# Full attention in reversed row order, with GpSimd marking zeros and the value sums made beforehand; router pieces moved in the windowed stage

## The chip, the cores and the metric

The kernel runs on one core of one Trainium2 chip. A core has five engines with instruction streams of their own: TensorE (PE in the profile; PEld is its weight load), VectorE (DVE), ScalarE (ACT), GpSimd (POOL) and SyncE (SP), and DMA queues. Each engine works through its stream in order and waits on semaphores. The metric is the device time of one execution in microseconds (us), as a median of several.

## The reference

A hidden state x of 2 x 2048 tokens by 128 features passes through four blocks in float32: windowed attention with 16 heads, a mixture of experts, full attention, and the same mixture of experts again. Each block adds to x what it makes of the normalised x. The change touches the routing of both mixtures and the full attention:

```python
# routing, before each mixture of 8 experts
logits = xf @ w_router
probs = jax.nn.softmax(logits, axis=-1)
topk_w, topk_idx = jax.lax.top_k(probs, 2)

# full attention: one head of width 128, 2 sequences of 2048
scores = jnp.einsum('bqd,bkd->bqk', q, k) / jnp.sqrt(jnp.float32(d_k))
scores = jnp.triu(scores, k=0)                       # a query sees itself and LATER keys
scores = jnp.where(scores == 0, -9000000000000000.0, scores)
attn = jax.nn.softmax(scores, axis=-1)
out = jnp.einsum('bqk,bkd->bqd', attn, v)
```

A zero score counts as masked, with a large finite value, so the masked keys ahead of a query still enter the sum with the weight that the softmax gives them.

## The kernel before, in words

Tokens lie in 32 tiles of 128 rows, in 8 groups of 4 tiles (512 tokens). The stages run one after the other; each is a block in which every engine has its own loop, written out by hand, and no scheduler moves anything.

**Windowed attention** (`window_stage`). `turn(sb, routed)` handles group sb: for each of 8 pairs of heads (c) it goes through 4 blocks (b), 32 steps (c, b) in all. Its first turn carries no routing, and the other seven route the group before (sb - 1) beside the attention. In a step PE makes scores (L627), transposes of probabilities (L637), one projection and the product with V (L650). DVE adds the mask and takes the extremum for the score tile made three steps ahead (L812, `maxima`), ACT exponentiates it (L734) and copies the transposes (L742). PE writes the next score tile only when `maxima` has emptied the bank, so a late DVE stops PE. In b = 1 and 2 DVE also swaps halves and multiplies by the cosine (L821, L825) for the rotary embedding, and POOL multiplies by the sine and adds (L962, L969), copies (L977, L984, L987), and every pair's last POOL work runs into the next pair's b = 0.

**The router** (`Router`) is a chain of small steps over one group of four tiles: `statistics` and `normalise` on DVE with a square root on ACT between them (`root`, L322, which needs another function table than the exponential), `turn` and `logits` on PE, `shift` on DVE, `exponentials` on ACT, `order`, `choose` and `accumulate` on DVE, `count` on PE, `assign` and `slots` on DVE, then on POOL `second` (L433, a copy) and `scatter` (L441, 8 indirect DMAs, two for each tile). Most DVE steps are links: an operation, then a wait for its own semaphore. In the windowed stage the step at which each piece runs is a pair (c, b) compared by hand: ROOT (2, 2), `normalise` (3, 0), TURN (3, 2), LOGITS (4, 0), EXPS (4, 1), `order` (4, 3), `choose` (5, 0), `accumulate` (5, 3), COUNT with `assign` and `slots` (6, 1), and the scatters in c = 6 and 7, four DMAs each. At LOGITS and COUNT PE waits for both halves of the latest score tile, since the small products share its bank.

**Full attention** (`full_stage`). For each of two batches: 12 projections (L1325, L1329), then 16 rows i of query tiles. Row i has the key tiles i to 15, cut into chunks of up to four tiles: 40 chunks in a batch, 136 tiles of scores. The rows go from i = 0 (four chunks) to i = 15 (one tile). The loop over chunks g is a pipeline:

- PE: `turn(g)` transposes the probabilities (L1347), `scores(g + 7)` (L1338), `values(g - 1)` multiplies by V (L1356). With the first chunk of each row it sums the value tile that has just become masked, by a product with ones (L1376).
- ACT: `copy(g + 6)` (L1415) takes the scores out of PSUM into U, `exponentials(g + 1)` (L1422, L1425), `read(g)` (L1432) copies the transposes.
- DVE: `take(g + 6)`: for a row's first chunk the triangle (L1492), then over the whole chunk u = (u == 0) - u (L1493) and a minimum over it (L1495); on the row's last chunk the bias for the exponential (L1498, L1499). `finish` of a row that is done (L1507 to L1523): add the new value sum to `pre`, add its masked share to the product, divide, add to x.
- POOL: the routing's copy and scatters only.

The bias of a row needs all chunks of it, and `values` of a row's first chunk waits until the row before the last has been finished.

The routing of the second mixture is spread over this loop: `ROUTE_AT[j]` is the chunk (of 80 over both batches) at which group j of finished rows begins, and STATS to SLOTS are steps 0 to 6 after it. Before the change the groups begin at 17, 29, 37, 45, 57, 69, 77 and 82; what is at 80 or later runs after the last chunk. PE's `routed` waits for a step's reader before the bank `pt` is written again. After the last scatter has landed the second expert stage starts.

## Time and profile before

| What | us |
|---|---|
| median of 3 runs (1600.51 to 1601.87) | 1601.13 |
| the profiled execution | 1602.77 |
| its span, from first to last instruction | 1601.0 |
| PE busy in the span | 1288.1 (80%) |
| DVE busy | 1065.4 (67%) |
| ACT busy | 912.0 (57%) |
| POOL busy | 787.3 (49%) |
| mean granted TensorE clock | 0.914 |

The shares are averages over stages with different limits. By the line numbers in the trace the windowed attention runs from about 57 to 843 us, the first expert stage from 875, the full attention from 1098 to 1398 and the second expert stage after it. A wait in the profile is idle time of one engine, with the engine whose signal ended it. "DVEq" is DVE's sequencer, which signals without an operation. The granted clock is a share of TensorE's 2.4 GHz.

### The profile page before, as it was taken

The numbers are of one execution on the slowest core, as the hardware profiler recorded it, in microseconds if no ns is written. First come the engines' busy times: TensorE is split into PE (matmuls) and PEld (weight loads), VectorE is DVE, ScalarE is ACT, GpSimd is POOL, SyncE is SP. The second block draws the span as 40 slices with busy tenths as digits, with TensorE's granted clock in tenths as the row PEclk, the third lists the DMA queues.
The fourth block names the chain that finished last, engine by engine and source line by source line (L and its number), as shares of the span: only waits on it lengthen the run. The fifth ranks groups of instructions, "written<-read, shape, count | busy, mean of one in ns | idle before, by whom it ended". The sixth has DMA issues, their size and how long they took to land. (4 is left out here: it accounts for less than half of the span.)

```text
span 1601.0 us, 34670 instructions
## 1 busy us (share of the span) xinstructions
PE 1288.1 (80%) x9684; PEld 1012.3 (63%) x9684; DVE 1065.4 (67%) x3751; ACT 912.0 (57%) x2312; POOL 787.3 (49%) x814
## 2 busy tenths in 40 slices
PE   0599999999999999999981888916978887188891
PEld 0477766766667676676751788913765666188891
DVE  5666777777767678776774455656886878445563
ACT  1377776768678686776852544513764666044450
POOL 4356667666676756757662344510022223434451
PEclk9899999999999999999995989967999899598896
DMA  5699994000000000000003112130000000121215
GB/s 191 120 210 205 202 207 90 1 9 6 1 15 0 15 1 7 8 1 15 1 12 135 58 54 59 56 106 0 1 14 14 14 16 25 34 64 55 59 57 158
DMA packets 129390, 91.84 MB, mean 57 GB/s; under 512 B 9115, under 2 KB 122030, under 8 KB 128992
## 3 DMA queue, kind: packets, MB, share of 16 engines
q1 hardware_dynamic: 118848, 71.32, 20.8%
q0 software_dynamic: 9248, 16.94, 3.2%
q10 hardware_dynamic: 1152, 2.13, 0.4%
q14 instruction: 106, 0.87, 0.2%
q8 instruction: 36, 0.59, 0.2%
HBM read 30.86 MB, written 61.64 MB: 58 GB/s over the span
## 5 line engine op out<-in xcount | busy, mean ns | idle before, releaser
L812 DVE CUSTOM_DVE_ANT_0 sc<-ps,mask 128x256 f32<-128x256 f32 x518 | 198.2, 420 | 155.8 <-PE ps L627 135.0
L734 ACT ACTIVATE sc<-sc,mx 128x256 f32<-128x256 f32 x516 | 257.6, 503 | 45.9 <-DVE mx L812 45.3
L962 POOL TENSOR_TENSOR rot<-rot,sin 128x512 f32<-128x512 f32 x132 | 180.3, 1366 | 202.0 <-DVE rot L821 202.0
L1107 POOL DMA_INDIRECT yt<-yo,xt x160 | 160.5, 1003 | 196.7 <-DVE yo L1207 168.1
L441 POOL DMA_INDIRECT xg<-r_xw,r_slot x128 | 127.5, 996 | 161.7 <-DVE r_slot L418 127.5
L627 PE MATMUL ps<-K,Q 64*128 64x256 f32 x1036 | 192.0, 433 | 15.7 <-DVE mx L812 15.7
L742 ACT COPY pT<-pt 128x512 f32<-128x512 f32 x257 | 150.3, 585 | 95.1 <-PE pt L637 86.5
L1167 ACT ACTIVATE hT<-ph,b 128x256 f32<-128x256 f32 x320 | 125.7, 477 | 86.6 <-PE ph L1130 86.6
L637 PE MATMUL pt<-ident,sc 128*128 128x128 f32 x1028 | 171.3, 290 | 1.6 <-ACT sc L734 1.3
L650 PE MATMUL po<-pT,V 128*64 128x128 f32 x2048 | 168.3, 285 | 0.0
L637 PEld LDWEIGHTS pt<-ident,sc 128*128 128x128 f32 x1028 | 109.9, 143 | 85.7 <-issue 52.0
L1148 PE MATMUL py<-w2s,hT 128*128 128x128 f32 x1280 | 161.6, 281 | 1.9 <-ACT hT L1167 1.8
L1148 PEld LDWEIGHTS py<-w2s,hT 128*128 128x128 f32 x1280 | 155.8, 198 | 2.7 <-ACT hT L1167 2.7
L650 PEld LDWEIGHTS po<-pT,V 128*64 128x64 f32 x2048 | 106.5, 136 | 65.9 <-issue 35.9
L1130 PE MATMUL ph<-xh,w1s 128*128 128x256 f32 x640 | 143.6, 307 | 0.0
L627 PEld LDWEIGHTS ps<-K,Q 64*128 64x128 f32 x1036 | 85.8, 186 | 61.1 <-issue 37.4
L1130 PEld LDWEIGHTS ph<-xh,w1s 128*128 128x128 f32 x640 | 112.5, 204 | 0.0
L825 DVE TENSOR_TENSOR lin<-lin,cos 128x512 f32<-128x512 f32 x132 | 108.0, 818 | 0.0
L734 ACT ACTIVATION_READ_ACCUMULATOR sc<-sc,mx 128x1 f32 x516 | 99.0, 192 | 0.0
L1162 ACT CAST xh<-px 128x256 fp32r<-128x256 f32 x80 | 29.9, 374 | 120.1 <-PE px L1121 78.3
L821 DVE STREAM_SHUFFLE rot<-lin 128x512 f32<-128x512 f32 x132 | 96.9, 734 | 0.2
L1189 DVE CAST w1s<-w1h 128x512 fp32r x80 | 34.0, 424 | 91.1 <-issue 90.1
(236 smaller groups left out, 2826.3 us busy)
## 6 DMA issues: line engine op xcount, KB each, us to landing
xg<-zeros SPq DMA_DIRECT2D x76, 520.0 KB, 10.1
xt<-xg SPq DMA_DIRECT2D x80, 130.0 KB, 2.1
got<-yt SPq DMA_DIRECT2D x32, 256.0 KB, 4.5
yt<-yo,xt POOLq DMA_INDIRECT x160, 2.3
x<-in_hidden SPq DMA_DIRECT2D x8, 256.0 KB, 8.2
xg<-r_xw,r_slot POOLq DMA_INDIRECT x128, 2.3
w<-in_w SPq DMA_DIRECT2D x1, 2048.0 KB, 8.7
out_x<-x SPq DMA_DIRECT2D x8, 256.0 KB, 3.9
```

The lines of the kernel that those rows point to most:

```text
L441: self.nc.gpsimd.indirect_dma_start(out=rows, out_offset=bass.IndirectOffsetOnAxis(ap=self.slot[:, self.buf(g), r, t:t + 1], axis=0), in_= ...
L627: ins = nc.tensor.matmul(ps[:, h, 0:2 * P], Q[r, c % QBUF, b * P:(b + 1) * P], K[r, c, b * P:(b + 2) * P], start=True, stop=True)
L637: ins = nc.tensor.transpose(pt[:, b % 2, h, kb, :], sc[:, b, h, kb * P:(kb + 1) * P], s.ident[:, :])
L650: ins = nc.tensor.matmul(po[h * HD:(h + 1) * HD, c % 2, b * P:(b + 1) * P], V[:, c, b + kb, h, :], pT[:, b % 2, h, kb, :], start=(kb == 0) ...
L734: nc.scalar.activation(sc[:, b, h, :], sc[:, b, h, :], ACT.Exp, scale=-1.0, bias=mx[:, b, h:h + 1], accum_out=ls[:, c % 2, b, h:h + 1]).th ...
L742: nc.scalar.copy(pT[:, b % 2, :, :, :], pt[:, b % 2, :, :, :]).then_inc(S["pt"], 1)
L812: nc.vector.tensor_tensor_reduce(sc[:, b, h, :], ps[:, h, 0:2 * P], (mask0 if b == 0 else mask)[:, :], -float(HD) ** -0.5, 3e38, ALU.add, ...
L962: nc.gpsimd.tensor_tensor(rot[:, which, :], rot[:, which, :], s.sin[:, pos(sb)], ALU.mult).then_inc(S["pool"], 1)
L1107: nc.gpsimd.indirect_dma_start(out=s.yt, out_offset=bass.IndirectOffsetOnAxis(ap=xt[:, k, r, HID:HID + 1].bitcast(U32), axis=0), in_=yo[:, ...
L1130: ins = nc.tensor.matmul(ph[:, k % 2, i, :], w[a], x[:, k % 2, :], start=(n == 0), stop=(n == 2))
L1148: ins = nc.tensor.matmul(py[:, k % 2, r * P:(r + 1) * P], hT[:, k % 2, i, r * P:(r + 1) * P], w2s[:, k % 2, i, :], start=(i == 0), stop=(i ...
L1167: nc.scalar.activation(hT[:, k % 2, i, :], ph[:, k % 2, i, :], ACT.Gelu_apprx_tanh, bias=s.b1[:, bass.ds(e * HCHUNKS + i, 1)]).then_inc(S[ ...
```

## The change

In the windowed stage the router's pieces stand at other steps: `normalise` (2, 3), LOGITS (3, 3), EXPS and `order` (4, 0), `choose` (4, 3), `accumulate` (5, 0), COUNT with `assign` (5, 2), `slots` (5, 3); of the eight scatters two stand in c = 5, two in c = 6 and four in c = 7.

In the full attention
- the rows go from i = 15 to i = 0, so that the one-chunk rows come first, and `Router` maps a group's number to its tiles by `where`;
- POOL applies the triangle (`mark`, new) and writes for every chunk a tile `flag` with 1 where the score is 0, in three buffers;
- DVE subtracts the flag and takes the maximum in one instruction (`tensor_tensor_reduce`), where it made two passes; the signs of the exponential follow;
- the 15 sums of value tiles are made ahead of the loop: four products of ones with four value tiles each (512 columns), and 15 linked additions on DVE (`sums`) into a tile for each row; `finish` no longer adds. The first seven score products stand ahead of them and after a wait for the last copy of V;
- the groups of the router begin at chunks 5, 13, 25, 43, 50, 57, 65 and 81, and the scatters are four steps (7 to 10) of two DMAs each in POOL's loop, which had no chunks in it before.

The core of the diff (left out: names of signals and buffers, `where` in `Router`, the index renamed on ACT and PE, the change of sign, the sizes of `pre` and `oo`, and the old lines of `take` and `finish`, which stand in the kernel above):

```diff
-        ROOT, TURN, LOGITS, EXPS, COUNT = (2, 2), (3, 2), (4, 0), (4, 1), (6, 1)
+        ROOT, TURN, LOGITS, EXPS, COUNT = (2, 2), (3, 2), (3, 3), (4, 0), (5, 2)
...
-                        if routed and (c, b) == (3, 0):
+                        if routed and (c, b) == (2, 3):
                             rt.normalise(dve, sb - 1)
+                        if routed and (c, b) == (4, 0):
+                            rt.order(dve, sb - 1)
                         if routed and (c, b) == (4, 3):
-                            rt.order(dve, sb - 1)
+                            rt.choose(dve, sb - 1)
                         if routed and (c, b) == (5, 0):
-                            rt.choose(dve, sb - 1)
+                            rt.accumulate(dve, sb - 1)
                         if routed and (c, b) == (5, 3):
-                            rt.accumulate(dve, sb - 1)
-                        if routed and (c, b) == COUNT:
                             rt.slots(dve, sb - 1)
...
+                    if routed and c == 5:
+                        pool.wait_ge(s.s_zeroed, 16 * ZERO_DMAS)
+                        rt.scatter(pool, sb - 1, (0,))
                     if routed and c == 6:
-                        pool.wait_ge(s.s_zeroed, 16 * ZERO_DMAS)
-                        rt.scatter(pool, sb - 1, (0, 1))
+                        rt.scatter(pool, sb - 1, (1,))
...
+        rt = Router(nc, m, s, 3, 2, 0, lambda j: BTILES // SB_TILES * (j // 4) + 3 - j % 4)
...
-        chunks = [[(k, min(4, BTILES - k)) for k in range(i, BTILES, 4)] for i in range(BTILES)]
-        first = [sum(len(c) for c in chunks[:i]) for i in range(BTILES + 1)]
+        rows = [(BTILES - 1 - r, [(k, min(4, BTILES - k)) for k in range(BTILES - 1 - r, BTILES, 4)])
+                for r in range(BTILES)]
+        first = [sum(len(chunks) for _, chunks in rows[:r]) for r in range(BTILES + 1)]
         NCH = first[-1]
-        chunk = [(i, c, k0, n) for i in range(BTILES) for c, (k0, n) in enumerate(chunks[i])]
+        chunk = [(r, i, c, k0, n) for r, (i, chunks) in enumerate(rows) for c, (k0, n) in enumerate(chunks)]
...
-        ROUTE_AT[3], ROUTE_AT[7] = NCH + 5, 2 * NCH + 2
-        END, MORE = 2 * NCH, 9
-        STATS, ROOT, NORMALISE, TURN, LOGITS, EXPS, CHOOSE, SUM, COUNT, SLOTS = 0, 0, 1, 2, 3, 3, 4, 5, 6, 6
+        ROUTE_AT[3], ROUTE_AT[4], ROUTE_AT[5], ROUTE_AT[7] = NCH + 3, NCH + 10, NCH + 17, 2 * NCH + 1
+        END, MORE = 2 * NCH, 12
+        STATS, ROOT, NORMALISE, TURN, LOGITS, EXPS, CHOOSE, SUM, COUNT, SLOTS, SCATTER = 0, 0, 1, 2, 3, 3, 4, 5, 6, 6, 7
...
+                for a in range(16):
                     if a >= 2:
-                        k = min(a - 1, 8)
-                        pe.wait_ge(S["qk"], START + 8 * b + k)
-                        if a - 1 > 8:
-                            pe.wait_ge(S["v"], START + 4 * b + a - 9)
+                        pe.wait_ge(S["qk"], START + 8 * b + min(a - 1, 8))
+                    if 10 <= a < 14:
+                        pe.wait_ge(S["v"], START + 4 * b + a - 9)
+                    if a >= 14:
+                        pe.wait_ge(S["pre"], START + 4 * b + a - 13)
                     if a < 2:
-                        pe.wait_ge(S["pre_sb"], START + (BTILES - 1) * b)
+                        pe.wait_ge(S["pre"], START + 4 * b)
+                    if a == 12:
+                        pe.wait_ge(S["v"], START + 4 * (b + 1))
+                        for g in range(AHEAD):
+                            scores(g)
...
+                    elif a >= 12:
+                        g = a % 4 * SB_TILES
+                        ins = nc.tensor.matmul(pp[:, a % 2, :], s.ones[:, :], V[:, g:g + SB_TILES, 0:HID],
+                                               start=True, stop=True)
                     else:
                         for t in range(SB_TILES):
                             g = a % 4 * SB_TILES + t
                             ins = nc.tensor.matmul(pp[:, a % 2, t * P:(t + 1) * P], xs[:, g * P:(g + 1) * P],
                                                    s.wb[:, 2 * HID:], start=True, stop=True)
                     ins.then_inc(S["proj"], 1)
...
-                    i, c, _, _ = chunk[g]
-                    if c == 0 and i > 0:
-
-                        pe.wait_ge(S["pre_sb"], START + (BTILES - 1) * b + max(i - 2, 0))
-                        nc.tensor.matmul(pp[:, i % 2, 0:HID + 1], s.ones[:, :], V[:, i - 1, :], start=True,
-                                         stop=True).then_inc(S["pre"], 1)
...
+                def sums(a):
+
+                    dve.wait_ge(S["proj"], START + 16 * b + a + 1)
+                    for t in range(SB_TILES):
+                        i = a % 4 * SB_TILES + t
+                        if i < BTILES - 1:
+                            ins = nc.vector.tensor_tensor(pre[:, i + 1, 0:HID], pre[:, i, 0:HID],
+                                                          pp[:, a % 2, t * P:(t + 1) * P], ALU.add)
+                            ch.link(ins)
+                    dve.sem_inc(S["pre"], 1)
+
                 def take(g):
 
-                    i, c, k0, n = chunk[g]
-                    if c == 0 and i >= UBUF:
-                        dve.wait_ge(S["p"], START + NCH * b + first[i - UBUF + 1])
-                    dve.wait_ge(S["copy"], START + NCH * b + g + 1)
+                    r, i, c, k0, n = chunk[g]
+                    if c == 0 and r >= UBUF:
+                        dve.wait_ge(S["p"], START + NCH * b + first[r - UBUF + 1])
+                    dve.wait_ge(S["flag"], START + NCH * b + g + 1)
                     to = U[:, g % UBUF, 0:n * P]
-                    if c == 0:
-
-                        ch.link(nc.vector.tensor_tensor(to[:, 0:P], to[:, 0:P], tri[:, :], ALU.mult))
-                    nc.vector.scalar_tensor_tensor(to, to, 0.0, to, ALU.is_equal, ALU.subtract).then_inc(S["u"], 1)
-                    dve.wait_ge(S["u"], START + NCH * b + g + 1)
-                    ch.mark(nc.vector.tensor_reduce(mn[:, i % UBUF, c:c + 1], to, AX_X, ALU.min))
-                    if c == len(chunks[i]) - 1:
-                        ch.wait()
-                        ch.link(nc.vector.tensor_reduce(st[:, i % UBUF, 0:1], mn[:, i % UBUF, 0:c + 1], AX_X, ALU.min))
-                        nc.vector.tensor_scalar(st[:, i % UBUF, 1:2], st[:, i % UBUF, 0:1], MASKED, None,
-                                                ALU.mult).then_inc(S["bias"], 1)
...
+                    top = mn[:, r % UBUF, c:c + 1]
+                    nc.vector.tensor_tensor_reduce(to, to, flag[:, g % FBUF, 0:n * P], 1.0, -3e38, ALU.subtract, ALU.max,
+                                                   top).then_inc(S["u"], 1)
+                    if c == len(rows[r][1]) - 1:
+                        dve.wait_ge(S["u"], START + NCH * b + g + 1)
+                        if c > 0:
+                            top = st[:, r % UBUF, 0:1]
+                            ch.link(nc.vector.tensor_reduce(top, mn[:, r % UBUF, 0:c + 1], AX_X, ALU.max))
+                        nc.vector.tensor_scalar(st[:, r % UBUF, 1:2], top, -MASKED, None, ALU.mult).then_inc(S["bias"], 1)
+
+                def finish(r):
+
+                    i = rows[r][0]
+                    dve.wait_ge(S["pv"], START + NCH * b + first[r + 1])
+                    dve.wait_ge(S["w0"], START + BTILES * b + r + 1)
+                    nc.vector.scalar_tensor_tensor(oo[:, r % 2, :], pre[:, i, :], st[:, r % UBUF, 2:3],
+                                                   po[:, r % 2, 0:HID + 1], ALU.mult, ALU.add).then_inc(S["o"], 1)
+                    dve.wait_ge(S["o"], START + BTILES * b + r + 1)
+                    ch.link(nc.vector.reciprocal(st[:, r % UBUF, 3:4], oo[:, r % 2, HID:]))
                     own = s.x[:, b * BTILES + i, :]
-                    ch.mark(nc.vector.scalar_tensor_tensor(own, oo[:, 0:HID], st[:, i % UBUF, 3:4], own,
+                    ch.mark(nc.vector.scalar_tensor_tensor(own, oo[:, r % 2, 0:HID], st[:, r % UBUF, 3:4], own,
                                                            ALU.mult, ALU.add))
 
                 for g in range(AHEAD - 1):
                     take(g)
+                for a in range(12, 16):
+                    sums(a)
...
+            def route(b, g):
+                for t in range(SB_TILES):
+                    for j in at(b, g, SCATTER + t):
+                        rt.scatter(pool, j, (t,))
+                for j in at(b, g, TURN):
+                    rt.second(pool, j)
+
+            for b in range(BATCH):
+                def mark(g):
+
+                    r, i, c, k0, n = chunk[g]
+                    pool.wait_ge(S["copy"], START + NCH * b + g + 1)
+                    of = U[:, g % UBUF, 0:n * P]
+                    if c == 0:
+                        nc.gpsimd.tensor_tensor(of[:, 0:P], of[:, 0:P], tri[:, :], ALU.mult).then_inc(S["tri"], 1)
+                        pool.wait_ge(S["tri"], START + 2 + BTILES * b + r + 1)
+                    pool.wait_ge(S["u"], START + NCH * b + max(g + 1 - FBUF, 0))
+                    nc.gpsimd.tensor_scalar(flag[:, g % FBUF, 0:n * P], of, 0.0, None, ALU.is_equal).then_inc(S["flag"], 1)
+
+                for g in range(AHEAD - 1):
+                    mark(g)
+                for g in range(NCH):
+                    if g + AHEAD - 1 < NCH:
+                        mark(g + AHEAD - 1)
+                    route(b, g)
+            for g in range(NCH, NCH + MORE):
+                route(1, g)```

DVE's stream in the windowed stage, from the steps (5, 3) to (6, 3) before (L395 is `accumulate`, L409 `assign`, L415 to L418 `slots`, L812 `maxima`, L821 and L825 the rotary work):

```order
L395 TENSOR_TENSOR r_acc<-r_acc,r_both 128x8
...
L844 TENSOR_TENSOR oT<-po,rT 128x512
...
L409 COPY r_acc<-r_acc 128x8
L410 TENSOR_TENSOR r_place<-ps,base 128x32
...
L812 ISA sc,mx<-ps,mask 128x256
...
L821 STREAM_SHUFFLE rot<-lin 128x512
...
L825 TENSOR_TENSOR lin<-lin,cos 128x512
L415 TENSOR_TENSOR r_picked<-r_hot,r_place 128x32
...
L418 CAST r_slot<-r_slotf 128x8
```

and after, from (5, 0) to (5, 3):

```order
L396 TENSOR_TENSOR r_acc<-r_acc,r_both 128x8
...
L839 RECIPROCAL rs<-ls 128x8
...
L410 COPY r_acc<-r_acc 128x8
L411 TENSOR_TENSOR r_place<-ps,base 128x32
...
L813 ISA sc,mx<-ps,mask 128x256
...
L826 TENSOR_TENSOR lin<-lin,cos 128x512
...
L813 ISA mx 128x1
L416 TENSOR_TENSOR r_picked<-r_hot,r_place 128x32
...
L419 CAST r_slot<-r_slotf 128x8
```

Each piece has moved two to five steps forward, and `slots` from behind the rotary work of (6, 1) to behind the maxima of (5, 3).

DVE's stream at the start of the full attention's first batch, before:

```order
L1480 COPY bV<-pp 128x4x128 x4
L1492 TENSOR_TENSOR U<-U,tri 128x128
L1493 SCALAR_TENSOR_TENSOR U<-U 128x512
L1495 TENSOR_REDUCE mn<-U 128x1
L1493 SCALAR_TENSOR_TENSOR U<-U 128x512
L1495 TENSOR_REDUCE mn<-U 128x1
```

and after:

```order
L1487 COPY bV<-pp 128x4x128 x4
L1509 ISA U,mn<-U,flag 128x128
L1509 ISA mn 128x1
L1516 TENSOR_SCALAR st<-mn 128x1
...
L1496 TENSOR_TENSOR pre<-pre,pp 128x128 x15
L1509 ISA U,mn<-U,flag 128x512
L1509 ISA mn 128x1
```

One pass and an accumulator read stand for two passes, and 15 additions stand between the first six chunks and the loop.

POOL's stream in the full attention, before, where each group is a copy and eight DMAs:

```order
L1541 UNCONDITIONAL_BRANCH
L1543 MEMSET tri 128x128
L1545 AFFINE_SELECT tri<-tri 128x128
L433 COPY r_xw<-r_xw 128x4x128
L441 DMA xg<-r_xw,r_slot 38912x130 x8
```

and after, around the scatter of the first group:

```order
L434 COPY r_xw<-r_xw 128x4x128
L1571 TENSOR_TENSOR U<-U,tri 128x128
L1574 TENSOR_SCALAR flag<-U 128x512 x2
L1574 TENSOR_SCALAR flag<-U 128x128
L1571 TENSOR_TENSOR U<-U,tri 128x128
L1574 TENSOR_SCALAR flag<-U 128x512 x2
L442 DMA xg<-r_xw,r_slot 38912x130 x2
L1574 TENSOR_SCALAR flag<-U 128x256
L442 DMA xg<-r_xw,r_slot 38912x130 x2
```

The DMAs have come to stand between instructions that DVE waits for.

## Rows read from the trace of the kernel before

**Rows 1.** Stretches: length, then busy PE, PEld, DVE, ACT, POOL; granted clock; DMA.

```profile
262.50:358.00 95.50, 91.87 (x735) 65.91 (x734) 71.55 (x252) 69.49 (x190) 65.49 (x69) 0.98 0.02 6
...
1120.60:1222.40 101.80, 84.41 (x540) 69.95 (x540) 83.72 (x291) 70.43 (x142) 16.25 (x17) 0.93 0.03 10
...
1242.40:1358.50 116.10, 93.65 (x571) 76.33 (x571) 94.14 (x373) 73.78 (x148) 32.48 (x34) 0.90 0.06 18
1358.50:1398.20 39.70, 6.14 (x29) 5.44 (x28) 17.47 (x107) 3.82 (x6) 18.13 (x20) 0.55 0.09 30
```

**Rows 2.** The waits of PE over five routed turns (total us, times, longest).

```profile
PE ps L627 <- DVE mx L812: 10.2, 10, 1.5
PE ps L400 <- DVE mx L812: 3.6, 5, 0.7
```

**Rows 3.** Timeline of PE at (6, 3) and later: start, us, idle before, releaser.

```profile
341.27 1.11 PE L627 MATMUL ps<-K,Q 64*128 64x256 f32 x4 [1.48 <-DVE mx L812]
...
343.22 1.91 PE L667 MATMUL pout<-wo,oT 128*128 128x128 f32 x8
...
355.19 1.06 PE L667 MATMUL pout<-wo,oT 128*128 128x128 f32 x8
```

**Rows 4.** The timelines of DVE, then of POOL, in the same turn.

```profile
297.11 0.42 DVE L812 CUSTOM_DVE_ANT_0 sc<-ps,mask 128x256 f32<-128x256 f32 x1 [2.37 <-PE ps L627]
...
329.31 3.15 DVE L395 TENSOR_TENSOR r_acc<-r_acc,r_both 128x8 f32<-128x8 f32 x4
...
339.76 1.06 DVE L418 CAST r_slot<-r_slotf 128x8 uint32<-128x8 f32 x1
...
329.13 1.27 POOL L962 TENSOR_TENSOR rot<-rot,sin 128x512 f32<-128x512 f32 x1
330.60 1.28 POOL L969 TENSOR_TENSOR K<-lin,rot 128x512 f32<-128x512 f32 x1 [0.20 <-POOL rot L962]
```

**Rows 5.** Groups by shape of DVE and POOL in the full attention (count | busy us, mean ns).

```profile
L1493 DVE SCALAR_TENSOR_TENSOR U<-U 128x512 f32<-128x512 f32 x56 | 38.6, 690 | 9.7 <-ACT U L1415 8.2 <-DVE r_acc L395 0.2
L1495 DVE TENSOR_REDUCE mn<-U 128x1 f32<-128x512 f32 x56 | 38.4, 686 | 1.9
...
L1492 DVE TENSOR_TENSOR U<-U,tri 128x128 f32<-128x128 f32 x32 | 9.3, 291 | 11.9 <-ACT U L1415 11.3
...
L1509 DVE TENSOR_TENSOR pre<-pre,pp 128x129 f32<-128x129 f32 x28 | 7.9, 282 | 0.3
...
L441 POOL DMA_INDIRECT xg<-r_xw,r_slot x56 | 55.8, 996 | 130.4 <-DVE r_slot L418 115.4 <-issue 14.9
L433 POOL COPY r_xw<-r_xw 128x512 f32<-128x512 f32 x8 | 4.9, 618 | 88.9 <-DVE r_xw L331 88.9
```

**Rows 6.** The page's costliest groups of the whole span.

```profile
L812 DVE CUSTOM_DVE_ANT_0 sc<-ps,mask 128x256 f32<-128x256 f32 x518 | 198.2, 420 | 155.8 <-PE ps L627 135.0
...
L962 POOL TENSOR_TENSOR rot<-rot,sin 128x512 f32<-128x512 f32 x132 | 180.3, 1366 | 202.0 <-DVE rot L821 202.0
```

**Rows 7.** The waits of PE from 1120.6 to 1358.5, both chunk loops.

```profile
PE bpt L1347 <- ACT U L1425: 18.4, 7, 3.5
PE bpt L400 <- DVEq L396: 12.5, 6, 3.5
...
PE bpt L1347 <- DVE r_slot L418: 4.6, 4, 1.6
```

**Rows 8.** The timeline of ACT at a group's step 0.

```profile
1157.40 1.28 ACT L322 ACT_TABLE_LOAD   x1
1160.86 0.21 ACT L322 ACTIVATE r_tmp<-r_tmp 128x4 f32<-128x4 f32 x1 [2.17 <-DVE r_tmp L318]
```

**Rows 9.** Timelines: PE before the first loop, DVE after the last chunk.

```profile
1111.88 6.43 PE L1338 MATMUL bps<-kT,qT 128*128 128x512 f32 x14
...
1364.60 0.87 DVE L309 BATCH_NORM_STATS2 r_stats<-x 128x6 f32<-128x128 f32 x4
...
1379.50 0.17 DVE L418 CAST r_slot<-r_slotf 128x8 uint32<-128x8 f32 x1
```

96 lines of the change are left out of this document (37 added, 59 removed).

## The prediction

> **What bounds the kernel now.** I read the table by stretches first, then PE's waits in the two stages that the change touches, and then the timelines around the longest of them.
>
> In a routed turn of the windowed stage PE is busy 91.9 of 95.5 us at a granted clock of 0.98, DVE 71.6, POOL 65.5 [rows 1]. PE bounds it, and what it loses it loses to a late `maxima`: 13.8 us over five turns, 2.8 us a turn, in stalls of up to 1.5 us at the score product and 0.7 at COUNT [rows 2]. The stall costs more than its length: after it the same product takes 1.91 us where a calm step has 1.06 [rows 3], so the granted clock had dropped to its lower level. The row shown lost 0.85 us by that; with the smaller products around it I put the loss at 1.5 us. Why is DVE late? Four tiny additions of `accumulate` take 3.15 us from 329.31 on, exactly while POOL's two multiplications run, 329.13 to 331.88, and the cast L418 takes 1.06 us there [rows 4] where it takes 0.17 in the full attention's tail [rows 9]. The two engines hold each other up. At (3, 0) on the other hand DVE had idled 2.37 us before its maxima [rows 4].
>
> In the full attention's two chunk loops PE is busy 84.4 of 101.8 us and 93.7 of 116.1, at clocks 0.93 and 0.90; DVE 83.7 and 94.1 [rows 1]. Neither engine is full. In [rows 7] PE's losses there have three causes: 18.4 us for the exponential in seven waits, 12.5 for `accumulate` before COUNT, 4.6 for the slots. They all hang on the router's pieces. The longest, 3.5 us [rows 7], is a group's step 0: ACT loads a table (1.28 us), waits 2.17 us for DVE's statistics [rows 8], and must load the exponential's table again. So DVE's passes are on the path only where they make such a piece late. From 1358.5 to 1398.2 there is nothing but the last group's chain [rows 1].
>
> **Part 1, the windowed stage.** `normalise` goes to (2, 3), into the idle 2.37 us: free. LOGITS and `shift` one step earlier, EXPS and `order` at (4, 0), where POOL idles: free, and if ACT's exponential comes late there DVE waits with its next maxima behind it; its cover is DVE's idle time, 24 of 95.5 us, 0.75 a step. `choose` goes to (4, 3), where POOL runs two long operations: each of its last linked steps may wait one operation of 1.37 us [rows 6], so the maxima of (5, 0) come up to 2 us later. The idle time of two steps, 1.5 us, covers most of it. I bound a new stall at 0 and 0.9 us and take 0.4. `accumulate` at (5, 0) runs beside POOL's short copies: free, and the COUNT wait of 0.7 goes. `slots` at (5, 3) takes the place of `accumulate` under the same two multiplications, and lasts as long, without a COUNT behind it: 0 to 0.5 us, I take 0.2. The stall of 1.48 us with the slow clock behind it goes, since (6, 1) has no `assign` or `slots` left. Per turn: -0.7 - 1.5 - 1.5 + 0.4 + 0.2 + 0.2 (a copy of `assign` beside POOL at (5, 2)) = -2.9. POOL's two DMAs at the end of c = 5 (0.996 us and their gap, (55.8 + 14.9) / 56 = 1.27 each, [rows 5]) push back its copies for c = 6 by 2.5 us, and the copy of x that the V projection needs; POOL's idle time, 30 of 95.5 us, is 3.7 us a pair and covers that. The DMAs of c = 6 are halved, those of c = 7 stay. Seven routed turns: 7 x 2.9 = **20 us less**, between 7 (every edge against it) and 29.
>
> **Part 2, the full attention.** DVE loses one pass in 80 chunks (56 of them at 0.686), 32 triangles at 0.291 and 28 additions to `pre` at 0.282 [rows 5]: 48 + 9 + 8 = 65 us; it gets 30 linked additions at 0.28 plus a wait that I put at 0.1, 11 us, and accumulator reads, 6. The pass that remains, with two inputs in SBUF, I price like L1493, 0.69; the same kind of instruction takes 0.42 for 256 columns in L812 [rows 6], 0.27 of it for the columns, which gives 0.69 too. So DVE has 48 us less over two batches. PE's work is the same within a microsecond (15 sums of 129 columns against 4 of 512 in each batch). What arrives on the path:
>
> - Before the first loop: the score products wait for V's last copy (+1.0), and PE's first transposes for the first 8 of 15 additions, which stand behind six chunks on DVE, themselves behind POOL. First scores at 1111.88 [rows 9], transposes at 1120.6 [rows 1]: 8.7 us now, about 11.3 then. With the fewer columns of scores done meanwhile, +3.5 a batch, **+7**; the rest of PE's work -1.
> - Short rows first: each row costs DVE about 1.2 us for bias and `finish` (two operations of 128 columns at 0.29, two tiny ones at 0.17, waits between them at 0.1), and `values` waits for the row before the last. PE's busy time at its clock, 84.4 x 0.93 + 93.7 x 0.90 = 163 us for 272 tiles [rows 1], is 0.6 us a tile with the router's share. In rows of one to four tiles PE so needs 0.6 to 2.4 us, DVE 1.6 to 2.0; and in batch 1 group 3 starts at chunk 3 there. +2 and +6, **+8**.
> - Router waits: table loads stay, so I let the 18.4 us fall to 14; COUNT's 12.5 to 5, slots and the rest by 2. **-13.5**; the lost clock, 0.07 x 101.8 + 0.10 x 116.1 = 19 us, shrinks with it by **-5**. Between the batches -1.
> - The end: before, the statistics of the last group start at 1364.60 [rows 9], 6.1 us after the last product at 1358.5, behind `finish` of several short rows and group 6's choice. Then one `finish` stands before them, some 1.3 us, and no other group's scatters delay its copy. **-6**.
> - POOL: a flag of 512 columns is not in the trace. A copy of one input takes 0.618 [rows 5], a two-input operation 1.37 [rows 6]. It has one input and a comparison, so I take 0.7. With the triangle (about 0.4) that is 34 x 0.7 + 16 x 0.4 = 30 us a batch, beside 32 DMAs at 1.27, 41 us: 71 of 100. In the four steps with DMAs POOL needs 3.2 us against PE's 2.4; it is ahead by two chunks in rows of four, which just covers it. **+2**.
>
> Sum: 7 - 1 + 8 - 13.5 - 5 - 1 - 6 + 2 = **-10 us** (-9.5), between +8 and -35.
>
> For the flags the Trainium skill has a rule that speaks against the change. "SBUF — State Buffer", section "Who interferes with whom", says that a DVE instruction with two SBUF inputs and a GpSimd instruction that reads SBUF exclude each other for the whole instruction. By that rule DVE's remaining pass (U and flag) and POOL's flag never overlap, and the trace agrees as far as [rows 4] show it. For the duration, "GPSIMD Engine Reference", section "Performance versus the Vector engine", measured 769 ns for 512 elements of a tight loop; with it the POOL sum would be 32 us a batch instead of 30, and the forecast the same.
>
> By the mechanism of [rows 4], the pass and the flag together need 0.69 + 0.7 = 1.4 us of a chunk of 2.4 us, as DVE's two passes did before; that is why I take so little of DVE's 48 us as gain.
>
> **The rivals.**
> A. *The forecast*: 1602.8 - 20 - 10 = 1573 of the profiled execution's own time, which lies 1.6 above the median, so 1571. 1558 to 1584.
> B. *DVE was the true bound of the full attention*, and the waits of [rows 7] almost vanish with its 48 us. For it: DVE is busy 83.7 of 101.8 us, and the waits of its many links come on top. Against it: the table loads, and PE's calm first chunks. Full attention -35: 1601 - 20 - 35 = 1546, 1538 to 1557.
> C. *The moves in the windowed stage only shift the stalls*: `choose` under POOL's multiplications stalls PE as `slots` did, and its clock drops. Windowed -3 to -7: 1601 - 6 - 10 = 1585, 1580 to 1600.
> D. *Slower: POOL becomes the bound.* A flag costs as much as a two-input operation, 1.37: 34 x 1.37 + 6 + 41 + 2 = 96 us a batch, in a loop of 100, and 4.1 us in each of 28 steps with DMAs against 2.4, less the cushion: +20. DVE's pass waits for a flag of 1.37 often enough for +19. The full attention gives 39 - 10 = +29, with -20 in the windows 1610; 1604 to 1625. It decides from about 1.2 us a flag. Against it: POOL's copy is at 0.618.
>
> **The numbers.** A 0.59, B 0.14, C 0.17, D 0.10. The predicted time is A's, 1571. 1548 to 1592 holds A, most of C and the upper half of B. A measurement of this kernel can tell about 0.2%, 3.2 us. Faster: A, B and 0.13 of C, 0.86; within 0.2%: the rest of C, 0.04; slower: D, 0.10.
>
> **What the profile after would show.** A routed turn of about 92.6 us instead of 95.5, PE's waits for `maxima` under 1.5 us a turn; if not, they stand at (5, 1). Flags of 512 columns at 0.6 to 0.8 us, some longer where DVE's pass ran. First transposes about 11 us after the first scores. COUNT's waits in the full attention at 5 us, and waits for the exponential still above 10. Statistics of the last group within 2 us of the last product. The forecast is wrong if the flag is above 1.2 us, if the exponential's waits vanish, or if windowed turns keep their 95.5.

## The result: slower by 63 us, and the profile after

The changed kernel takes 1664.46 us (median of four runs, 1659.45 to 1667.07), the kernel before 1601.5 beside it: 1.0389 of its time, 95% interval 1.0367 to 1.041. Forecast were 1571 us, and the time lies outside the range of 1548 to 1592, on the side to which only rival D pointed, and beyond D's own 1604 to 1625. The profiled execution has a span of 1657.7 us (1601.0 before).

First the stretches of the changed kernel, as in [rows 1]: a routed turn, the start of batch 1 in full attention, its chunk loop, the chunk loop of batch 2, the end. Columns: stretch, length, busy PE, PEld, DVE, ACT, POOL, granted clock, DMA share, GB/s.

```profile
262.50:358.00 95.50, 93.09 (x761) 66.85 (x760) 73.33 (x256) 70.48 (x192) 67.75 (x71) 1.00 0.02 7
...
1090.00:1120.70 30.70, 23.73 (x71) 11.40 (x72) 11.65 (x51) 10.12 (x20) 11.14 (x14) 0.83 0.00 1
1120.70:1254.00 133.30, 94.10 (x524) 74.39 (x523) 61.23 (x288) 69.80 (x140) 79.29 (x70) 0.83 0.04 12
1281.90:1420.80 138.90, 97.94 (x539) 76.97 (x537) 69.56 (x338) 74.46 (x146) 88.58 (x79) 0.86 0.05 16
1420.80:1453.70 32.90, 4.10 (x19) 3.63 (x18) 11.88 (x70) 2.39 (x5) 8.38 (x9) 0.58 0.06 19
```

The chunk loops take 133.3 and 138.9 us where they took 101.8 and 116.1 [rows 1]. VectorE did lose its work, 84 us busy down to 61 in batch 1, and it bought nothing: GpSimd went from 16 busy us to 79, PE's clock from 0.93 to 0.83, and no engine is full.

The whole stage, from the first and to the last product of PE's timeline:

```profile
1089.95 9.72 PE L1344 MATMUL pp<-xT,wb 128*128 128x512 f32 x16 [1.08 <-PEq L151]
...
1104.49 3.75 PE L1325 MATMUL bps<-kT,qT 128*128 128x128 f32 x12 [0.88 <-DVE bV L1487]
...
1109.58 1.88 PE L1347 MATMUL pp<-bV,ones 128*128 128x512 f32 x4
1117.13 3.75 PE L1347 MATMUL pp<-bV,ones 128*128 128x512 f32 x4 [5.68 <-DVEq L1499]
1120.67 0.42 PE L1362 MATMUL bpt<-ident,U 128*128 128x128 f32 x1
...
1418.80 2.00 PE L1371 MATMUL bpo<-bV,bpT 128*128 128x129 f32 x16
```

I call **F** the time from the first of these to the end of the last: 330.8 us. In the kernel before the same two points are 1098.37 and 1358.35, so F was 260.0. Of the 70.8 us more, PE stands still for 49 (94 for 45) and is busy 22 longer (236.9 for 215.3) with much the same work at a granted clock of 0.85 for 0.92. The 56.7 us between the two spans are then: 8.4 less ahead of the stage, 70.8 more in F, 5.1 less from its end to the router's total (19.6 to 14.5), and 0.6 less elsewhere.

The waits of PE, VectorE (DVE) and GpSimd (POOL) in the stage, 1090 to 1421 (us in total, times, longest), to be held against [rows 7], which begin with the first chunk loop and so leave out the start of batch 1 (here that start adds 5.6 us to the row of L1347 and 6.1 to VectorE's wait for flags):

```profile
PE bpt L1362 <- ACT U L1431: 32.7, 11, 10.2
PE bpt L401 <- DVEq L397: 22.5, 7, 4.4
PE bpt L340 <- DVE r_xw L332: 12.9, 6, 3.0
PE pp L1347 <- DVEq L1499: 11.2, 2, 5.7
PE bpt L1362 <- DVE r_sh L359: 8.1, 5, 3.2
...
DVE U L1509 <- POOL flag L1574: 128.2, 55, 4.6
...
POOL U L1571 <- ACT U L1421: 63.9, 17, 15.1
POOL flag L1574 <- ACT U L1421: 57.7, 24, 6.0
```

PE's waits for exponentials, forecast to fall from 18.4, rose to 32.7. VectorE stands 128 us before flags. But GpSimd is not simply full either: it stands 122 us before ScalarE's copies. L1431 is the exponential, L401 the router's COUNT, r_xw its normalised tokens, r_sh its shifted logits. And the groups by shape from 1090 to 1454, the stage and the last group's row writes (count | busy us, mean ns | idle before):

```profile
L1574 POOL TENSOR_SCALAR flag<-U 128x512 f32<-128x512 f32 x56 | 85.8, 1532 | 43.2 <-ACT U L1421 40.6
L442 POOL DMA_INDIRECT xg<-r_xw,r_slot x64 | 70.5, 1102 | 26.1 <-issue 16.0 <-DVE r_slot L419 10.1
L1509 DVE CUSTOM_DVE_ANT_0 U<-U,flag 128x512 f32<-128x512 f32 x56 | 40.8, 729 | 102.1 <-POOL flag L1574 100.3 <-DVE r_acc L396 1.1 <-DVE pre L1496 0.4
L1571 POOL TENSOR_TENSOR U<-U,tri 128x128 f32<-128x128 f32 x32 | 15.1, 471 | 64.5 <-ACT U L1421 63.9 <-DVE mn L1509 0.5
```

A flag of 512 columns takes 1.53 us, not 0.7. How the parts work together is seen at the longest wait, PE's 10.2 us. The timelines of POOL, DVE, ACT and PE around it:

```profile
1206.00 1.52 POOL L1574 TENSOR_SCALAR flag<-U 128x512 f32<-128x512 f32 x1
1207.70 1.47 POOL L442 DMA_INDIRECT xg<-r_xw,r_slot  x1 [0.18 <-issue]
1209.48 0.96 POOL L442 DMA_INDIRECT xg<-r_xw,r_slot  x1 [0.30 <-issue]
1210.47 2.34 POOL L1574 TENSOR_SCALAR flag<-U 128x512 f32<-128x512 f32 x2
...
1212.02 0.88 DVE L1509 CUSTOM_DVE_ANT_0 U<-U,flag 128x512 f32<-128x512 f32 x1 [3.77 <-POOL flag L1574]
...
1216.47 0.20 ACT L323 ACTIVATE r_tmp<-r_tmp 128x4 f32<-128x4 f32 x1 [9.80 <-DVE r_tmp L319]
...
1218.91 0.47 PE L1362 MATMUL bpt<-ident,U 128*128 128x128 f32 x1 [10.23 <-ACT U L1431]
```

POOL issues two row writes, then makes the next flag. VectorE waits 3.77 us for that flag for a chunk that lies six steps ahead; behind it in VectorE's queue stand the row's end and the router's statistics, 4.4 us of work once the flag is there. ScalarE waits 9.80 us for the statistics, with the next exponential behind, and PE waits 10.23 us for that exponential. So there are two suspects: the row writes ahead of the flag in GpSimd's queue, and the flag ahead of the router in VectorE's.

### The profile page after: what moved, and what is told of

It reads as the page before. It is cut to its first block and busy times, and to the rows that moved or that the text cites. A ratio compares the mean times of both kernels' runs of the same rounds, so it can differ in the third digit from the quotient of the medians.

```text
span 1657.7 us, 34802 instructions
## 1 busy us (share of the span) xinstructions
PE 1307.8 (79%) x9640; PEld 1018.6 (61%) x9640; DVE 1022.8 (62%) x3727; ACT 907.7 (55%) x2312; POOL 917.9 (55%) x926
## 5 line engine op out<-in xcount | busy, mean ns | idle before, releaser
L813 DVE CUSTOM_DVE_ANT_0 sc<-ps,mask 128x256 f32<-128x256 f32 x518 | 198.6, 421 | 161.6 <-PE ps L628 137.4
L963 POOL TENSOR_TENSOR rot<-rot,sin 128x512 f32<-128x512 f32 x132 | 183.7, 1391 | 184.9 <-DVE rot L822 184.9
L628 PE MATMUL ps<-K,Q 64*128 64x256 f32 x1036 | 192.9, 434 | 15.0 <-DVE mx L813 15.0
L442 POOL DMA_INDIRECT xg<-r_xw,r_slot x128 | 134.1, 1047 | 63.1 <-issue 32.6
L1574 POOL TENSOR_SCALAR flag<-U 128x512 f32<-128x512 f32 (+2 forms) x80 | 106.7, 1337 | 60.9 <-ACT U L1421 57.7
L1509 DVE CUSTOM_DVE_ANT_0 U<-U,flag 128x512 f32<-128x512 f32 (+2 forms) x80 | 53.0, 665 | 130.2 <-POOL flag L1574 128.2
L628 PEld LDWEIGHTS ps<-K,Q 64*128 64x128 f32 x1036 | 86.6, 187 | 60.4 <-issue 34.8
L826 DVE TENSOR_TENSOR lin<-lin,cos 128x512 f32<-128x512 f32 x132 | 109.7, 831 | 0.0
L1371 PEld LDWEIGHTS bpo<-bV,bpT 128*128 128x128 f32 x544 | 82.1, 215 | 36.3 <-issue 29.1
```

The source lines that it names most:

```text
L442: self.nc.gpsimd.indirect_dma_start(out=rows, out_offset=bass.IndirectOffsetOnAxis(ap=self.slot[:, self.buf(g), r, t:t + 1], axis=0), in_= ...
L628: ins = nc.tensor.matmul(ps[:, h, 0:2 * P], Q[r, c % QBUF, b * P:(b + 1) * P], K[r, c, b * P:(b + 2) * P], start=True, stop=True)
L813: nc.vector.tensor_tensor_reduce(sc[:, b, h, :], ps[:, h, 0:2 * P], (mask0 if b == 0 else mask)[:, :], -float(HD) ** -0.5, 3e38, ALU.add, ...
L963: nc.gpsimd.tensor_tensor(rot[:, which, :], rot[:, which, :], s.sin[:, pos(sb)], ALU.mult).then_inc(S["pool"], 1)
```

## The experiments

Each ratio is to the kernel before on the same chip, with its 95% interval. "Window edits" are those of the windowed stage; all kernels below have them. F is read from the profile of each kernel as above, that is from one execution. The four or more times of one kernel in these experiments lie 3 to 17 us apart, and in the 18 traces with the window edits the full attention begins anywhere from 1084.7 to 1100.3; so a difference of a few us in F, or between two medians, is not shown by itself.

**1. The window edits alone.** The kernel before with

```diff
-        ROOT, TURN, LOGITS, EXPS, COUNT = (2, 2), (3, 2), (4, 0), (4, 1), (6, 1)
+        ROOT, TURN, LOGITS, EXPS, COUNT = (2, 2), (3, 2), (3, 3), (4, 0), (5, 2)
```

and the matching places of VectorE's pieces and GpSimd's writes.

> The kernel before with the windowed stage's edits alone (positions of the router's products, of VectorE's pieces and of GpSimd's row writes); full attention as before. In the trace of after, a routed turn took 94.07 us against 95.5, and full attention began 8.4 us earlier. If these edits stand alone, the kernel takes 1593 us (1590 to 1596), 0.5% under before, with 2.4 to 3 us of PE's waits moved, not removed. Rival (the gain was a by-product of something else, or is given back in full attention, whose first products then meet the same waits): 1600 to 1603.

1596.17 us, ratio 0.9934 (0.9914 to 0.9955), F 259.8. The edits stand alone and are worth about 11 us by the runs (7 to 14). The loss lies in full attention.

**2. VectorE marks the zeros again** and applies the triangle, in the passes of before, all else as changed. The core of the edit:

```diff
-                    nc.vector.tensor_tensor_reduce(to, to, flag[:, g % FBUF, 0:n * P], 1.0, -3e38, ALU.subtract, ALU.max,
-                                                   top).then_inc(S["u"], 1)
+                    nc.vector.scalar_tensor_tensor(to, to, 0.0, to, ALU.is_equal, ALU.subtract).then_inc(S["u"], 1)
+                    dve.wait_ge(S["u"], START + NCH * b + g + 1)
+                    ch.mark(nc.vector.tensor_reduce(top, to, AX_X, ALU.min))
```

> The changed kernel with the zeros marked by VectorE again, in two passes of a chunk (triangle multiply 0.29 us, two-input pass 0.69, minimum 0.69), and nothing of it on GpSimd but the row writes; last row first, sums made beforehand, router positions as changed. Theory 1 (the flag on GpSimd, in series between ScalarE's copy and VectorE's pass, is the loss): the kernel falls to the level of before or below it, 1593 us (1580 to 1608). Theory 3 (the row order and the longer start of a batch cost most of the 63 us): it stays at 1625 or more.

1620.84 us, 1.0119 (1.0084 to 1.0155), F 290.2. Between the two expectations: flags and triangles on GpSimd cost 40.6 us of F, net of the pass that VectorE saves by them, the rest of the full-attention change 30.4.

**3. The router ahead of the chunk in VectorE's queue**:

```diff
-                    if g + AHEAD - 1 < NCH:
-                        take(g + AHEAD - 1)
                     if g >= 2 and chunk[g - 2][0] != chunk[g - 1][0]:
                         finish(chunk[g - 2][0])
                     route(b, g)
+                    if g + AHEAD - 1 < NCH:
+                        take(g + AHEAD - 1)
```

> The changed kernel, but in each step of full attention VectorE first finishes the row and does the router's pieces, and then takes the chunk that lies six ahead, for which it waits for GpSimd's flag. No work is added or removed. Theory 1 (order in the queue: VectorE stands 122 us before flags with the router's pieces and the row's end behind it, and PE and ScalarE stand for those): the router's waits of PE (22.5 + 12.9 + 8.1 us) and ScalarE (25.1 + 17.2) fall by half, the kernel by 15 to 30 us to 1635 to 1650. Theory 2 (GpSimd's amount of work is the bound): within 5 us of 1664.

1634.29 us, 1.0173 (1.0158 to 1.0188), F 294.7. Two lines exchanged give back 36 us of F and 35 of the whole by the two ratios. The waits of PE, then of DVE, from 1088 to 1391 in its trace:

```profile
PE bpt L1362 <- ACT U L1431: 26.5, 10, 9.7
PE bpt L401 <- DVEq L397: 26.2, 7, 5.9
PE pp L1347 <- DVEq L1499: 11.2, 2, 5.7
...
DVE U L1509 <- POOL flag L1574: 71.8, 39, 4.0
```

VectorE's wait for flags fell from 128 to 72 us. The fall came elsewhere than expected, though: COUNT's wait (L401) did not halve, it grew from 22.5 to 26.2; what went are PE's waits for r_xw (12.9 to 1.2) and r_sh (8.1 to 2.1), and for exponentials (32.7 to 26.5), and the clock of batch 1 rose from 0.83 to 0.89. Of the 36 us, 24 are less standing of PE and 12 less busy time (236.9 to 224.8).

**4. A flag at the price of the prediction**: GpSimd marks 3/8 of a chunk.

```diff
-                    nc.gpsimd.tensor_scalar(flag[:, g % FBUF, 0:n * P], of, 0.0, None, ALU.is_equal).then_inc(S["flag"], 1)
+                    nc.gpsimd.tensor_scalar(flag[:, g % FBUF, 0:n * P * 3 // 8], of[:, 0:n * P * 3 // 8], 0.0, None, ALU.is_equal).then_inc(S["flag"], 1)
```

> The changed kernel, with GpSimd marking only the first 3/8 of each chunk (192 of 512 columns; the other flags are a constant zero, so zeros there are not moved to the mask's value). The flag then takes about 0.7 us, the value of the prediction, in place of 1.5; triangle, waits and all else stay. Theories 1 and 2 (time of the flag, in series or as GpSimd's load): some 80 flags less by 0.75 us at one in one to one in two on the path, so 30 to 60 us less, 1605 to 1635. If the prediction's other steps hold, it comes to 1571 to 1585. Theory 3 (row order and start): under 15 us less, 1650 or more.

1628.75 us, 1.0146 (1.013 to 1.0163), F 292.3, within 2.1 us of experiment 2. A flag of 192 columns took 0.72 us. At that price the move to GpSimd costs next to nothing, but it gains nothing either, though VectorE has one pass a chunk less than in experiment 2.

**5. The other order of VectorE's queue in the kernel that does not wait for flags**: the exchange of experiment 3 in experiment 1's kernel, to see whether the gain there belonged to the flags.

> The kernel before with the windowed edits (as e1_window_only, 1596), and in full attention VectorE finishes the row and does the router's pieces before it takes the chunk six ahead. Theory A (the order in VectorE's queue costs wherever it waits): PE's router waits (22.2 + 6.0 + 3.9 us in e1_window_only) fall by 5 to 10 us, 1588 (1584 to 1592). Theory B (it costs only where the flag comes late; with its own two passes VectorE hardly waits before a chunk, and here the router's pieces push the passes back, so PE's 18.3 us before exponentials grow by as much): 1594 to 1600.

1585.41 us, 0.9873 (0.9832 to 0.9914), F 246.5. Theory A, then: the gain does not belong to the flags, 13 us of F are won in the kernel before as well. The chunk loops of experiments 1 and 5 (of each the stretch of batch 1, then of batch 2):

```profile
1115.60:1216.10 100.50, 84.02 (x539) 69.77 (x540) 82.50 (x287) 70.16 (x142) 15.26 (x16) 0.93 0.03 10
1237.30:1353.10 115.80, 94.28 (x570) 77.68 (x570) 93.95 (x372) 73.78 (x148) 32.30 (x34) 0.88 0.06 18
```

```profile
1117.00:1212.20 95.20, 82.11 (x538) 68.65 (x539) 81.59 (x287) 69.82 (x142) 15.87 (x16) 0.95 0.03 10
1236.90:1344.50 107.60, 87.81 (x558) 73.37 (x556) 91.92 (x379) 71.90 (x145) 35.16 (x36) 0.92 0.06 21
```

**6. The sums beforehand alone**: as experiment 2, but rows from first to last and the router's positions of before.

```diff
-        rows = [(BTILES - 1 - r, [(k, min(4, BTILES - k)) for k in range(BTILES - 1 - r, BTILES, 4)])
+        rows = [(r, [(k, min(4, BTILES - k)) for k in range(r, BTILES, 4)])
                 for r in range(BTILES)]
...
-        ROUTE_AT[3], ROUTE_AT[4], ROUTE_AT[5], ROUTE_AT[7] = NCH + 3, NCH + 10, NCH + 17, 2 * NCH + 1
+        ROUTE_AT[3], ROUTE_AT[7] = NCH + 5, 2 * NCH + 2
```

> As e2_dve_flags (windowed edits, value sums made beforehand, VectorE marks the zeros), but rows from first to last and the router's positions of before. Against e1_window_only it differs in the sums beforehand alone. e2_dve_flags stood 25 us above e1_window_only. Theory A (longer start of a batch, 28.4 and 25.8 us against 22.3 and 19.9, is the sums'; the slower body is the row order's): +9 to +13 us, 1605 to 1609. Theory B (the row order is innocent, the sums cost nearly all): 1617 to 1622.

1609.17 us, 1.0016 (0.9987 to 1.0044), F 273.4. The sums cost 13.6 us of F, all of it and more in the starts of the batches (30.4 and 29.1 us against 22.3 and 19.9), and the row order, with the router's positions that go with it, 16.8 more, as theory A had it.

**7. Experiment 2 with the router ahead.**

> e2_dve_flags with VectorE's router pieces ahead of the chunk. With e3_route_first it makes the pair that differs only in who marks the zeros. If the 14 us between e2_dve_flags (1620.8) and e3_route_first (1634.3) are the flag's own remaining cost, this stays at 1615 to 1622; if e3_route_first merely gained what any kernel gains by that order (some 30 us), this falls below 1600.

1593.45 us, 0.9927 (0.9897 to 0.9956), F 262.1. It fell below 1600, by 27 us (28 of F), where the kernel with flags had fallen by 30 (36 of F). So the two effects add in the main: the order of VectorE's queue is worth 28 to 36 us of F with reversed rows whoever marks the zeros, and the flags are worth 33 to 41 in either order.

**8. The flags with rows from first to last**, router ahead.

> e3_route_first (GpSimd marks, sums beforehand, router pieces ahead of the chunk) with rows from first to last and the router's positions of before. Theory A (the reversed rows cost some 14 to 18 us by themselves): 1617 to 1622. Theory B (with short rows last, the four-chunk rows first: the first exponential waits for four flags in a row of 1.5 us and the start grows by as much): 1630 to 1640.

1634.2 us, 1.0177 (1.0132 to 1.0223), F 295.7, one microsecond off experiment 3. The time is theory B's, but the reason it gave is not borne out: the two starts grew by 4 us together (32.5 and 30.1 for 30.7 and 28.1), not by 14 to 18. With the router ahead, reversing the rows costs nothing net, and the equality hides a trade: with rows from first to last PE stands 45.9 us before exponentials (26.5 in experiment 3) and 12.3 before COUNT (26.2). The profiled execution here was the slowest of its four, 9 us above their median. With VectorE's two passes F of experiment 7 is 15.6 above experiment 5; if the sums cost their 13.6 there too, 2 are left for the row order. So what the row order cost in experiment 6 it cost mostly through the order of VectorE's queue.

**9. Flags that nobody reads**: experiment 7, and GpSimd runs flags and triangles on a tile of ones.

> e7_dve_flags_route_first (1593.5), and GpSimd runs the same 80 flags and 32 triangles as in the changed kernel, at the same points of its queue, but on a tile of ones, and nobody reads what it writes. Added work, no added wait. Theory B (contention: an operation on GpSimd makes VectorE's two-input passes and row ends wait, or longer; or the row writes, now behind flags, come too late): as slow as e3_route_first, 1625 to 1640, with VectorE's passes longer than 0.69 us. Theory A (the loss is VectorE's wait for the flag): within 5 us of e7, 1589 to 1598.

1615.95 us, 1.0096 (1.0076 to 1.0116), F 280.0: 18 us of F more with not one wait for a flag, so theory A of that expectation is wrong in its "within 5 us", and theory B's 1625 to 1640 was not reached either. VectorE was busy 12 us longer, mostly in small operations: a cast of the router (L419) took 0.57 us and a two-input one (L417) 0.63, where they take 0.17 and 0.18 alone.

```profile
1178.24 0.63 DVE L417 TENSOR_TENSOR r_picked<-r_hot,r_place 128x32 f32<-128x32 f32 x1
1178.90 0.22 DVE L418 TENSOR_REDUCE r_slotf<-r_picked 128x8 f32<-128x64 f32 x1
1179.16 0.57 DVE L419 CAST r_slot<-r_slotf 128x8 uint32<-128x8 f32 x1
...
1178.21 1.49 POOL L1581 TENSOR_SCALAR flag<-same 128x512 f32<-128x512 f32 x1 [0.18 <-POOL flag L1581]
```

The last line is POOL's, in the same microseconds. This kernel has VectorE's two passes and GpSimd's load together, which the changed kernel has not, so the 18 us can't be carried over to it; the longer operations show that contention exists. The row writes stand behind flags here as well, and what of the 18 us is theirs was not separated.

**10. No row writes**: experiment 3 without the 64 writes of the second router.

```diff
         for t in tiles:
+            if self.nth == 1:
+                pool.sem_inc(self.put[self.buf(g)], 16 * TOPK)
+                continue
             for r in range(TOPK):
                 self.nc.gpsimd.indirect_dma_start(
```

> e3_route_first (1634.3) without the 64 indirect row writes of the second router, which full attention's GpSimd queue holds at 1.1 us each (the expert stage then computes on rows that were never written; only full attention's length is to be read). Theory A1 (GpSimd's queue: a flag waits behind two row writes of a step, 2.2 us, and the flags arrive late in those steps): full attention, from its first product to the last product of values, falls from 294.7 us by 15 to 30 us. Theory A2 (the time from ScalarE's copy to the flag, 1.5 to 2 us, in every step, whatever else is queued): by under 8 us.

F 252.9, 41.8 us less than experiment 3 (the time of the whole, 1570.8, also holds an expert stage that works on other rows). In its trace VectorE waited for flags

```profile
DVE U L1512 <- POOL flag L1577: 38.9, 38, 3.4
```

instead of 71.8 us.

**11. Eight chunks ahead in place of seven** in experiment 3 (`AHEAD = 8`).

> e3_route_first with products, copies, flags and takes eight chunks ahead of the transposes in place of seven (11 buffers for 10). Work is equal, VectorE's and GpSimd's leeway before the exponentials grows by a step of some 2.8 us. Theory A2 (a chunk's longer way through GpSimd takes up the lead): PE's 25 us of waits for exponentials fall by more than half, the kernel by 10 to 20 us to 1614 to 1624. Theory A1 (GpSimd behind by its amount of work at the places where it waits for nothing): under 6 us, 1628 to 1640; and a start of a batch that is longer by 1 to 3 us, for one more flag comes before the sums.

1621.22 us, 1.0124 (1.0107 to 1.0141), but F 292.3, 2.4 us less than experiment 3; the rest of the difference lies ahead of the stage, where both kernels are the same (it begins at 1085.2 here and at 1094.9 there). PE's waits for exponentials fell to 14 us and others came, so a longer lead alone does not cure it.

**12. The small flag with the router ahead.**

> e3_route_first with GpSimd marking only the first 3/8 of each chunk (0.7 us for 1.5; the other flags are a constant zero). In the order of the changed kernel this gave 36 us. If the loss hangs on the flag's length and not on there being a hand-over: the same here, 1597 to 1603, 4 to 10 us above e7_dve_flags_route_first (1593.5). If the hand-over between engines is itself the loss, it stays above 1615.

1594.41 us, 0.9939 (0.9915 to 0.9963), F 261.5, the same as experiment 7 (262.1). Again: at 0.7 us the flags cost nothing, at 1.5 us they cost 33 of F. It is not the hand-over between engines that costs, it is the length, here together with the row writes in the same queue: without them (experiment 10) flags of full length cost nothing either.

**13. No flags and no writes**: experiment 7 without row writes.

> e7_dve_flags_route_first without the 64 indirect row writes of the second router (the expert stage then computes on rows never written; only full attention is to be read). Full attention, first product to last product of values, was 266.3 us with them, and 294.7 in e3_route_first; without them e3_route_first came to 253.0 (e10_no_row_writes). Theory Q (the flags queue behind the writes: the writes cost only where flags are on GpSimd): 262 to 266 us here, and GpSimd's flags without writes cost nothing any more. Theory W (the writes cost of themselves, by slowing VectorE's small operations as GpSimd's flags did): 240 to 252 us, and the flags' cost is not the queue's.

F 261.6. (The 266.3 us in this expectation is a slip; experiment 7's F is 262.1, from 1088.17 to 1350.25.) The writes by themselves cost 0.5 us of F, nothing that can be told from zero. Behind VectorE's two passes they are free, ahead of flags they cost 42: theory Q. And experiment 10 against this one shows the other side: without writes, flags on GpSimd are 8.7 us of F *faster* than two passes on VectorE, 5 us by the two ratios (0.9815 and 0.9848), whose intervals overlap. It is the only pair in which VectorE's saved pass seems to bring something. The last product of values in both traces, this one first:

```profile
1350.43 2.00 PE L1374 MATMUL bpo<-bV,bpT 128*128 128x129 f32 x16
```

```profile
1338.71 2.00 PE L1374 MATMUL bpo<-bV,bpT 128*128 128x129 f32 x16
```

(They began at 1090.79 and 1087.83.)

**14. The writes one in a step over eight steps** in experiment 3, not two over four.

> e3_route_first, with the second router's row writes issued one in a step over eight steps, not two in a step over four. GpSimd's work is equal. A step with two writes holds GpSimd 0.46 + 1.5 + 2.2 = 4.2 us, with one 3.1, against a step of some 2.8 us. Theory Q (peaks of GpSimd's queue delay the flags): PE's waits for exponentials (25.1 us) fall by 8 to 15 us, the kernel to 1618 to 1628. Theory W: within 4 us of 1634 (one group's buffer comes free a step late, up to 3 us either way).

1606.21 us, 1.001 (0.9992 to 1.0029), F 275.5: the same work on GpSimd, 19 us less of F and 26 of the whole by the ratios, level with the kernel before. Theory Q again, and more than it expected.

**15. Eight ahead in experiment 5's kernel.**

> e5_window_route_first (1585.4, the fastest so far: windowed edits, and in full attention the router's pieces ahead of the chunk, VectorE's two passes, rows from first to last) with eight chunks ahead in place of seven. PE stood 14.9 us before exponentials there. If VectorE's lead is what these waits lack: 1576 to 1582. If they stand where VectorE works without pause (its amount of work, 94 of 116 us in the second batch), a longer lead only moves them, and the start of each batch is 1 to 3 us longer: 1584 to 1590.

1578.76 us, 0.9847 (0.9825 to 0.987), F 242.6, as the first of the two expectations had it; by F and by the ratios the gain over experiment 5 is only 4 us, with intervals that overlap. The fastest kernel of the study, 25 us under the kernel before.

**16 and 17. The edits of experiments 14 and 10 in the changed kernel itself**, its own order of VectorE's queue kept.

> The changed kernel itself (its own order of VectorE's queue), with the second router's row writes issued one in a step over eight steps instead of two over four. In e15_one_write_a_step the same edit took 19 us off full attention (294.7 to 275.5) where the router's pieces stand ahead. Theory Q (a flag behind two writes is what costs in the changed kernel too): full attention, first product to last product of values, falls from 330.9 to 305 to 315 us and the kernel to 1636 to 1650. Theory L (in this order VectorE waits for every flag with the router behind it, whether a write is ahead of the flag or not; spreading writes makes more steps late): 322 us or more, 1655 to 1670.

1656.35 us, 1.0318 (1.0288 to 1.0347), F 325.1.

> The changed kernel itself without the second router's 64 row writes (the expert stage then computes on rows never written; only full attention is to be read). e2_dve_flags, the same kernel with VectorE's two passes, took 290.2 us for full attention, the changed kernel 330.9. Theory Q: 282 to 295 us, the flags cost nothing without the writes. Theory L (the flag's own time in VectorE's order costs): 305 us or more.

F 313.6. Both results lie where theory L put them (322 or more, 305 or more), but the writes are not free here either. Spreading them gives 5.7 us of F, leaving them out 17.2, and 23.4 us stay above experiment 2 with no write on GpSimd at all. (Experiment 2 has the writes. Without flags they cost 0.5 us with the router ahead; in this order that was not run.) VectorE still stood 110 us before flags in experiment 17:

```profile
DVE U L1512 <- POOL flag L1577: 110.1, 52, 4.6
```

So with the chunk ahead of the router, the larger part of the flags' cost is the flag's own time (theory L); with the router ahead, it is the full flag and the row writes together in GpSimd's queue (theory Q), for there neither the full flag without writes (252.9) nor the small flag with them (261.5) costs anything.

F of the kernels with reversed rows and sums beforehand, in one table:

| F, us | two VectorE passes | flags, no row writes | flags and row writes | 3/8 flags and row writes |
|---|---|---|---|---|
| chunk ahead of router (as changed) | 290.2 | 313.6 | **330.8** | 292.3 |
| router ahead of chunk | 262.1 | 252.9 | 294.7 | 261.5 |

Without the row order and the sums, F is 260.0 before, 259.8 with the window edits, 246.5 with the router ahead too, and 242.6 with eight ahead.

## Why the prediction was wrong

The forecast span was 1571.5 us, the measured one is 1657.7. Of these 86 us the flags hold 39, the other terms inside F 36, and the windowed stage with what follows it 12. So two steps failed, about equally.

**The flag, the step that failed first.** The prediction took 0.7 us "between" a copy and a two-input operation, because a flag has one input, and gave POOL +2. It measured 1.53, above both ends of the bracket (0.618 and 1.37). With 1.53 it is 40.6 of the 70.8 us. With 0.7 us it would have been 2.1 (experiment 4) or nothing (experiment 12), but that this meets the +2 is luck: the measured numbers are net of the pass that VectorE saves, and the forecast had that gain in other terms (-13.5 and -5 for waits and clock), where none of it came. The prediction said "wrong if the flag is above 1.2 us", and it was; the chance of 0.10 for that was far too low for a duration that no row showed. Rival D's +39 for the flags (20 by POOL's steps with writes, 19 by VectorE's waits) was near the 40.6, and its two mechanisms can be told apart in experiment 17: 17 us go with the writes, 23 stay without them.

Beside it, the Trainium skill, page "GPSIMD Engine Reference", section "Performance versus the Vector engine", gives 769 ns for 512 elements in a tight loop. That is its best case and no figure for a comparison. In this case's trace the comparison of 512 columns took 1.53 us, twice that.

A second step of the prediction bears on this: that pass and flag never overlap and together need 1.4 us of a chunk. In the changed kernel VectorE's pass of 512 columns means 0.729 us against 0.69, some 2 us over 56 passes, and the flags 1.53 against 1.49 in calm steps, 2 us more. They do overlap; what VectorE lost, it lost by standing before flags.

**The terms besides the flag: -5.5 inside F (-11.5 with the end) were forecast, +30.4 came.** Even rival D came out at 1610 since it kept them. Experiment 2 holds them: F 290.2 against 259.8. It gives VectorE its second pass back, so what the saved pass may have earned is not in this number but in that of the flags.

- *Start of a batch, +7.* The sums and the later V gave +6.1 and +5.9 us in experiment 2 (28.4 and 25.8 against 22.3 and 19.9), and +8.4 and +8.2 with flags: 12 to 17 over both batches. First transposes came 16.2 us after the first scores, not 11.3. The prediction counted VectorE's additions; it missed that PE's second pair of sum products waits for the first bank to be read (5.68 us in the lines above) and then takes 3.75 us itself ahead of the transposes. In the kernel before, such products lay between chunks.
- *Short rows, +8.* In the chunk loops, from the first transposes to the last values, the reversed rows cost 22.0 us (114.0 and 122.1 in experiment 2 against 97.9 and 116.2 in experiment 6), and 5.2 less in the starts. Experiment 8 and experiments 5 and 7 speak against VectorE's work a row, as priced, and for its order: with the router ahead the cost all but goes, in the net.
- *Router waits, -13.5, and clock, -5.* Both rose. PE's waits for exponentials went from 18.4 to 32.7, for COUNT from 12.5 to 22.5, for r_xw from 2.9 to 12.9, and the clock fell from 0.93 and 0.90 to 0.83 and 0.86. Here lies the deepest error: the prediction saw that these waits "all hang on the router's pieces" and then let them shrink with VectorE's busy time. They hang on what stands ahead of the pieces in VectorE's queue. Experiment 5 takes no work away and gets F down by 13; the change took 43 us of VectorE's busy time away (1065.4 to 1022.8 over the span) and put a longer wait in front.
- *The end, -6.* Right: 5.1. The statistics start 1.0 us after the last product (1421.81).
- *Between batches, -1.* Right: before, PE's projections of batch 2 began 0.9 us after the last values of batch 1 (1221.61 to 1222.53), now they follow at once (1253.80).

**The windowed stage, -20 (7 to 29).** Measured about 11 by experiment 1, inside the range and half the size. A turn of the changed kernel takes 94.05 us (COUNT's products at 234.08 and, six turns later, 798.37) against 95.5, not 92.6. The same code takes 93.5 to 95.3 us a turn in the 18 traces that hold it, 94.4 in the mean, which makes 8 us over seven turns; and full attention begins at 1090.2 in their mean, 8 us earlier than in the one trace of before. The COUNT wait went, and so did the drop of the clock (1.00 for 0.98). What failed is the "+0.4 for `choose` at (4, 3)": the stall moved there whole. PE's waits for maxima over five turns are 9.6 us (10.2 before, [rows 2]), and they stand here:

```profile
323.74 1.32 DVE L390 TENSOR_TENSOR r_hot<-iota,r_tf 128x32 f32<-128x32 f32 x1
325.09 0.20 DVE L392 TENSOR_TENSOR r_both<-r_hot 128x32 f32<-128x32 f32 x1
...
323.73 1.28 POOL L942 TENSOR_TENSOR xl<-xT,xh  x1
...
326.15 1.04 PE L628 MATMUL ps<-K,Q 64*128 64x256 f32 x4 [1.26 <-DVE mx L813]
```

A tiny step of `choose` takes 1.32 us beside an operation of POOL where its neighbour takes 0.20, the maxima come late, PE stands 1.26 us. That is rival C's mechanism, in part. It was told as a rival and priced too low in the forecast.

**What stays open.** Why the parts of the two queues' costs do not simply add (17 us for the writes in one order, 42 in the other) was not followed step by step. The windowed edits gave 7 to 14 us in the runs of experiment 1 and 8 in the mean of the traces; its own trace shows less (turns of 95.1, the stage 5.1 us earlier), and why turns of one code differ by up to 1.8 us was not looked into. How much of a flag's cost is its time and how much its contention with VectorE's small operations (experiment 9) was not separated in the changed kernel.

## To carry to other kernels

Before work goes to an idle engine, ask for the duration of that very kind of instruction there, and where no row has it, let the other end of the bracket be as likely as the hoped one (here the duration lay beyond it). An in-order engine that waits for something six steps ahead makes everything behind it wait too: put what others need now ahead of what is needed later (13 us here for two exchanged lines, and 28 to 36 with reversed rows). Long issues that nobody waits for, such as row writes, were free where nothing awaited stood behind them (0.5 us) and dear ahead of awaited flags (42 us of F, 19 of which came back by spreading them).

## What the runs showed of the hardware

- A comparison with a constant on GpSimd costs more than a copy and no less than a two-input operation (1.37, [rows 6]): 0.540, 0.920, 1.186 and 1.532 us for 128, 256, 384 and 512 columns, 1.49 in calm steps; a copy of 512 columns is at 0.618 [rows 5].
- VectorE's pass over two tiles and GpSimd's flag do run at the same time, but not freely. Of the 56 passes of 512 columns in experiment 3's trace 13 take 0.8 to 1.09 us and most others 0.69. The first two below lie within flags, the third began with its flag (VectorE's lines first, then GpSimd's):

```profile
1130.97 0.98 DVE L1509 CUSTOM_DVE_ANT_0 U<-U,flag 128x512 f32<-128x512 f32 x1 [0.77 <-POOL flag L1574]
1134.68 1.09 DVE L1509 CUSTOM_DVE_ANT_0 U<-U,flag 128x512 f32<-128x512 f32 x1
...
1291.45 0.69 DVE L1509 CUSTOM_DVE_ANT_0 U<-U,flag 128x512 f32<-128x512 f32 x1
...
1129.45 2.62 POOL L1574 TENSOR_SCALAR flag<-U 128x512 f32<-128x512 f32 x2
...
1132.77 3.33 POOL L1574 TENSOR_SCALAR flag<-U 128x512 f32<-128x512 f32 x2
...
1291.45 2.03 POOL L1574 TENSOR_SCALAR flag<-U 128x512 f32<-128x512 f32 x1
```

The Trainium skill, "SBUF — State Buffer", section "Who interferes with whom", says that a VectorE instruction with two inputs in SBUF contends with a GpSimd instruction that reads SBUF, and calls their shared ports an exclusive lock. The traces here show no lock for a whole instruction. Where the flag was there first, the pass took 0.3 to 0.4 us more, never a whole flag more. Where the two began together, at 1291.45, the pass kept its 0.69 us and the flag took 2.03 in place of 1.49, less than the 2.18 that one after the other would need. Flags are not needed for it: in experiment 7 five of VectorE's passes take 0.98 to 1.10 us beside GpSimd's copy for the router.

- An indirect write of 128 rows occupies GpSimd 1.09 to 1.10 us in kernels with flags (experiment 3, the changed kernel) and 0.99 us without (experiment 7), and 0.16 to 0.30 us pass before each.
